# Attention masks: q minus k formed on TensorE, 1024 columns a mask instruction, middle value parts on VectorE

## The chip, the core and the metric

One core of a Trainium2 chip runs one program with five engines, each with its own in-order queue: TensorE (PE; its weight loads are shown as PEld), VectorE (DVE), ScalarE (ACT), GpSimd (POOL) and SyncE (SP), which here issues DMAs. Engines wait for each other on semaphores. The metric is the device time of one execution in microseconds (us); lower is better.

## The reference

Four blocks follow each other, each added to a residual stream after a layer norm: an attention without softmax (16 batches of 256 tokens, 16 heads of 8), a mixture of 32 experts, an RWKV block and a mixture of 8 experts. Only the first is changed. Cut to what matters:

```python
q_proj, k_proj = proj(q), proj(k)          # gelu(x @ W1 + b1) @ W2 + b2: one number a token and head
std = sqrt(0.5 * (var_q + var_k) + eps)    # over the tokens of a batch
q_proj, k_proj = (q_proj - mean_q) / std, (k_proj - mean_k) / std
Z = concatenate([k_proj, q_proj]); idx = argsort(Z)
vc = v - mean(v)                           # v centred over the tokens
# prefix sums in sorted order, read at the query positions:
context = q * sum(vc[k <= q]) - sum((vc * z)[k <= q])
norm = 2 * (q * count(k <= q) - sum(z[k <= q])) - (q * T - sum(z))
context = 2 * context / max(norm, 1e-4)
```

So each query needs sums of 18 columns a head (8 values, a 1, 8 values times k, k) over the keys that are not above it. The kernel makes a 0/1 mask of keys by queries for each head and multiplies it with these columns on TensorE. The columns go in as three bf16 parts (high, middle, third), so that their sum has float32 accuracy.

## The kernel before

`build` runs `attention0`, `routed` (32 experts), `rwkv` and `routed` (8 experts), each as blocks of five hand-written engine programs with a barrier between blocks. `attention0` has two blocks.

The first block: VectorE takes row statistics of x and writes normed rows to `h_tok` (`normed`, L498), a half (16 tiles of 128x128) at a time; TensorE turns them, makes q and k, turns those to feature-major; then a loop over 8 groups of 512 tokens (`step`, L411 to L433) multiplies by Wv, W1 and W2. The product with W2 lands on 64 partitions of one PSUM tile for q (`down["q"]`) and of another for k, and VectorE adds b2 to each and takes statistics (L559 to L567). v is centred by VectorE (L549) and turned back by TensorE. In this block GpSimd fills four small tiles (L373 to L377), and ScalarE fills `pick` and 64 rows of `q_parts` (L439 to L444). SyncE loads weights, then clears the sorted-row buffers of later blocks.

The second block begins with a preparation: VectorE turns the statistics into 1/std, then a loop over 16 batches writes `qn` and `kn` (L631, L633), TensorE turns them (L829), ScalarE copies `q_parts`, a rounded `hi_r` and the token-major `q_tok`, `k_tok` (L708 to L713), and GpSimd writes the rest of q (L762). After that TensorE sums k (L834).

Then comes the main loop, one pass a batch, software-pipelined by one batch. For four heads at a time (a quad) TensorE spreads q over all 128 partitions: four matmuls with `pick` as weights (L850) fill a 128x1024 PSUM tile. Quads 0 and 1 become masks on VectorE, one compare of 128x1024 for each half of the keys (L651). Quads 2 and 3 become masks on ScalarE, a Sign of 128x256 for each head and half of the keys (L735), with values -1, 0, 1; for these heads the columns are weighted by a half (`head_weight`, `part_weight`) and TensorE adds a matmul by ones (L867). 64 matmuls of 128x54 (L876) multiply masks and value parts, VectorE sums the three parts (L662), GpSimd forms numerators (L797, L799), and VectorE divides and takes statistics (`results`, L672 to L683). Beside that GpSimd makes the next batch's columns and their remainders (L776 to L789), and ScalarE writes the high and the middle bf16 part (L742, L749). All this stands in register loops of two batches. The order in each queue is as written in `step` and the loops: for VectorE masks of quad 0, sums of the batch before, masks of quad 1, results of the batch before; GpSimd's numerators stand just ahead of them in time.

## Time and profile before

| | us |
|---|---|
| three runs | 1201.04, 1202.76, 1203.92 (median 1202.76) |
| span of the profiled execution, first to last instruction | 1200.0 |
| first block of the attention, to the start of the group loop | 60.4 |
| group loop | 44.5 |
| second block, preparation | 26.1 |
| second block, main loop and its end | 171.5 |
| everything after the attention | 897.6 |

A span leaves out what lies before the first and after the last instruction; the profile gives no time of its own for that execution beside the span, so the median of the runs stands 2.76 us above the span. In the rows below times are us from the start of the span, unless ns is named. A row of the timeline has start, duration, engine, line, operation, output and inputs, count, and in brackets the idle time before it with what ended it. Several instructions in a row are merged (x4), and their duration runs from the start of the first to the end of the last.

### The profile page before, as it was taken

How to read it: one execution, taken by the hardware profiler on the slowest of the kernel's cores; microseconds unless marked ns; L12 is line 12 of the kernel's file. 1: busy time of each engine (PE TensorE's matmuls, PEld its weight loads, DVE VectorE, ACT ScalarE, POOL GpSimd, SP SyncE). 2: the span in 40 equal slices, each digit the busy share in tenths (PEclk: the TensorE clock that was granted, in tenths of full speed). 3: DMA queues.
4: the chain of work that ended last, by engine and by line, in shares of the span. 5: the costliest groups of instructions: out<-in, count | busy, mean ns of one | idle time of the engine just before them, and what ended most of it. 6: DMA issues, size and time to landing. Idle time of an engine off the chain costs nothing. (4 is left out here: it accounts for less than half of the span.)

```text
span 1200.0 us, 20045 instructions
## 1 busy us (share of the span) xinstructions
PE 872.6 (73%) x5732; PEld 699.2 (58%) x5732; DVE 765.0 (64%) x2389; ACT 658.5 (55%) x1352; POOL 513.8 (43%) x634
## 2 busy tenths in 40 slices
PE   3796567675238999986995366777668989999910
PEld 2633455554227889975993133444457979999900
DVE  5479688887775457212676799998868641115636
ACT  4355777776635225653664676776775645555500
POOL 0002555555226666667774773000005663035155
PEclk9998777777557999997997688798867999999965
DMA  7960000000601126645763110000031133223132
GB/s 210 289 181 0 1 0 0 0 0 1 249 17 41 47 65 193 194 139 161 197 166 95 49 49 18 1 0 1 1 142 46 43 113 91 65 82 89 40 97 61
DMA packets 133845, 97.01 MB, mean 81 GB/s; under 512 B 11649, under 2 KB 125697, under 8 KB 132737
## 3 DMA queue, kind: packets, MB, share of 16 engines
q1 hardware_dynamic: 121472, 70.79, 19.7%
q0 software_dynamic: 12288, 25.19, 7.2%
q8 instruction: 42, 0.69, 0.2%
q14 instruction: 43, 0.34, 0.1%
HBM read 45.61 MB, written 50.33 MB: 80 GB/s over the span
## 5 line engine op out<-in xcount | busy, mean ns | idle before, releaser
L1122 POOL DMA_INDIRECT e_xs<-h_tok,rows_of x128 | 128.4, 1003 | 104.1 <-DVEq L1615 35.4
L735 ACT ACTIVATE mask<-ps_q,k_neg 128x256 bf16<-128x256 f32 x256 | 100.7, 488 | 34.8 <-PE ps_q L850 34.8
L1135 POOL DMA_INDIRECT e_got<-e_ys,e_rows_of x64 | 66.2, 1035 | 115.6 <-DMA e_ys<-e_y_rows 87.5
L850 PE MATMUL ps_q<-q_parts,pick 128*128 (+1 forms) x256 | 59.2, 367 | 50.0 <-DVE mask L651 41.6
L1778 DVE TENSOR_TENSOR e_hidden<-e_ps_gu,e_hidden 128x512 f32<-128x512 f32 x48 | 33.2, 691 | 96.8 <-ACT e_hidden L1461 96.6
L1271 PE MATMUL e_ps_gu<-e_w_all,e_x_turned 128*128 x384 | 92.0, 383 | 0.1
L1466 ACT ACTIVATE e_hidden<-e_ps_up 128x512 f32<-128x512 f32 x80 | 47.8, 597 | 73.4 <-PE e_ps_up L1309 73.2
L1122 POOL DMA_INDIRECT e_xs<-h_tok,e_rows_of x64 | 66.3, 1035 | 49.7 <-DVEq L1615 19.8
L1326 PE MATMUL e_ps_y<-e_w_all,e_h_turned 128*128 x640 | 84.2, 275 | 0.0
L2283 POOL DMA_INDIRECT c_got<-e_ys,rows_of x64 | 69.8, 1090 | 30.3 <-issue 19.2
L651 DVE TENSOR_TENSOR mask<-ps_q,k_tok 128x1024 bf16<-128x1024 f32 x64 | 75.1, 1214 | 9.2 <-PE ps_q L850 7.2
L850 PEld LDWEIGHTS ps_q<-q_parts,pick 128*128 128x128 f32 x256 | 45.0, 245 | 57.2 <-issue 40.0
L1326 PEld LDWEIGHTS e_ps_y<-e_w_all,e_h_turned 128*128 128x128 f32 x640 | 77.6, 192 | 0.0
L1271 PEld LDWEIGHTS e_ps_gu<-e_w_all,e_x_turned 128*128 128x128 f32 x384 | 70.0, 192 | 8.4 <-issue 0.7
L1135 POOL DMA_INDIRECT e_got<-e_ys,rows_of x64 | 65.1, 1017 | 21.3 <-issue 17.4
L1098 POOL MEMSET e_ones_bf<- 128x128 bf16 x2 | 0.4, 204 | 156.8 <-POOLq L1904 154.5
L1461 ACT ACTIVATE e_hidden<-e_ps_gu 128x512 f32<-128x512 f32 x48 | 28.7, 598 | 55.5 <-PE e_ps_gu L1271 55.5
L2322 PE MATMUL c_ps_f<-c_f_mix_k,c_ffn_Wk 128*128 128x512 f32 x64 | 44.4, 832 | 16.7 <-DVE c_f_mix_k L1959 15.3
L2295 PE MATMUL c_ps_t<-ident,y_tok 128*128 128x128 f32 x64 | 13.1, 339 | 57.0 <-ACT y_tok L2216 29.4
L1793 DVE COPY e_y_rows<-e_ps_y 128x512 f32<-128x512 f32 x20 | 13.8, 691 | 62.4 <-PE e_ps_y L1326 62.4
L1290 PE MATMUL e_ps_ring<-e_w_all,e_h_turned 128*128 x384 | 50.8, 276 | 0.0
L662 DVE TENSOR_REDUCE sums<-ps_o 128x144 f32<-128x432 f32 x64 | 34.4, 599 | 23.0 <-PE ps_o L876 23.0
(410 smaller groups left out, 2597.4 us busy)
## 6 DMA issues: line engine op xcount, KB each, us to landing
e_x_rows<-e_xs SPq DMA_DIRECT2D x68, 256.0 KB, 2.9
e_ys<-e_y_rows SPq DMA_DIRECT2D x68, 256.0 KB, 2.4
e_xs<-zeros SPq DMA_DIRECT2D x2, 6144.0 KB, 34.2
e_w_all<-in_w SPq DMA_DIRECT2D x4, 1536.0 KB, 13.0
e_xs<-zeros SPq DMA_DIRECT2D x2, 2560.0 KB, 27.5
e_w_all<-in_w SPq DMA_DIRECT2D x4, 1024.0 KB, 11.0
x_tok<-in_x SPq DMA_DIRECT2D x4, 512.0 KB, 6.0
e_xs<-h_tok,rows_of POOLq DMA_INDIRECT x128, 2.3
```

The source lines that it names most:

```text
L651: last = nc.vector.tensor_tensor(mask[parity][quad][j][:, :].rearrange("p (h t) -> p h t", t=T), psq[0][:, :].rearrange("p (h t) -> p h t" ...
L662: last = nc.vector.tensor_reduce(sums[:, o:o + HALF * VC].rearrange("p (h r) -> p h r", r=VC), pso[u * 2 + half][:, 0:HALF * HV].rearrange ...
L735: last = nc.scalar.activation(mask[u][QS // 2 + j][keys][:, h * T:(h + 1) * T], psq[1][:, h * T:(h + 1) * T], ACT.Sign, bias=k_neg[u][:, k ...
L850: last = nc.tensor.matmul(psq[0 if on_dve else 1][:, h * T:(h + 1) * T], pick[:, (quad * HQ + h) * P:(quad * HQ + h + 1) * P], q_parts[:, ...
L1122: nc.gpsimd.indirect_dma_start(out=xs[part], out_offset=bass.IndirectOffsetOnAxis(ap=rows_of[:, t * K + k:t * K + k + 1], axis=0), in_=til ...
L1135: nc.gpsimd.indirect_dma_start(out=got[t % GB][:, k * P:(k + 1) * P], out_offset=None, in_=ys[part], in_offset=bass.IndirectOffsetOnAxis(a ...
L1271: last = nc.tensor.matmul(ps_gu[n % 2][:, t * 2 * P:(t + 1) * 2 * P], x_turned[n % 2][:, t * P:(t + 1) * P], at(w_all, col, 2 * P), start= ...
L1290: last = nc.tensor.matmul(bank_y(n)[:, o], h_turned[n % TB][:, o], at(w_all, col + 2 * P, P), start=True, stop=True)
L1326: last = nc.tensor.matmul(bank_y(q)[:, t * P:(t + 1) * P], h_turned[n % TB][:, i * P:(i + 1) * P], at(w_all, col + (CH1 + i) * P, P), star ...
L1466: nc.scalar.activation(hidden[n % HB][:, :], ps_up[n % 2][:, :], ACT.Silu).then_inc(t_hidden, 1)
L2283: nc.gpsimd.indirect_dma_start(out=got[t % GB][:, k * P:(k + 1) * P], out_offset=None, in_=env["ys0"], in_offset=bass.IndirectOffsetOnAxis ...
L2322: last = nc.tensor.matmul(ps_f[j % 2][:, :], mats["ffn_Wk"][:, i * P:(i + 1) * P], f_mix["k"][:, :], start=True, stop=True)
```

## The change

q and k are kept in one tile: W2's products go to partitions 0 to 63 (q) and 64 to 127 (k) of one PSUM tile, and are added to b2, measured and normed together. Both variances are added by one small matmul with the constant `both`. In chunks of two batches ScalarE writes a rounded copy `hi_r` (zero or negated, by row), GpSimd adds it to the value (`parts`), SyncE stores the 128x512 tile to a DRAM tensor and loads 16 pieces of it back into `q_wide` and `k_wide`. In these, each strip of 32 partitions has four rows in use: two for the parts of k (with -1 opposite) and two for the parts of q (with 1 opposite), so that a matmul over 32 rows gives q minus k for 128 keys and 256 queries. GpSimd fills the constants of these tiles in the first block. A ScalarE mask is one Sigmoid of 128x1024 with a scale of 2 to the 60. Quads 1 to 3 go to ScalarE (six such units a batch), quad 0 to VectorE, which compares q with k as before. VectorE, no longer ScalarE, copies the middle value parts; VectorE's results come two batches late instead of one. The weights of a half, the matmuls by ones, `pick` and `q_parts` are gone. Sums are taken in two halves of eight heads, with one PSUM bank for each half of the queries. The loops are written out for all 16 batches instead of register loops. PSUM: two tiles of 128x1024 for ScalarE (`psa`), one for VectorE (`psd`), two banks for the products.

Cut to what is spoken of below:

```diff
-        q_parts = sb("q_parts", N, F32R)
-        pick = sb("pick", HEADS * P, F32R)
...
+        q_wide, k_wide = ([sb(f"{n}_wide{i}", SLOTS * 2 * CW, F32R) for i in range(2)] for n in "qk")
...
                 @block.gpsimd
...
+                    def constant(ins):
+                        ins.then_inc(consts_made, 1)
+                        pool.wait_ge(consts_made, next(made))
...
+                    for x in (*q_wide, *k_wide, q_only):
+                        constant(nc.gpsimd.memset(x[:, :].bitcast(F32), 0.0))
+                    for r in range(RG):
+                        rows = slice(r * HR, r * HR + 4)
+                        for i in range(2):
+                            constant(nc.gpsimd.memset(q_wide[i][rows, :].bitcast(F32), -1.0))
+                            constant(nc.gpsimd.memset(k_wide[i][rows, :].bitcast(F32), 1.0))
+                        constant(nc.gpsimd.memset(q_only[rows, :].bitcast(F32), 1.0))
+                        constant(nc.gpsimd.memset(q_only[r * HR:r * HR + 2, :].bitcast(F32), 0.0))
...
-                                nc.tensor.matmul(down[x][0:PR, :], w2[:, :], gelu[x][:, :],
+                                nc.tensor.matmul(down[ROWS_OF[x], :], w2[:, :], gelu[x][:, :],
...
+                        nc.vector.tensor_scalar(at(proj, g * GW, GW), down[:, :], b2[:, :], None,
+                                                ALU.add).then_inc(pr_sb, 1)
...
+                @block.sync
+                def _(sp):
+                    def store(c):
+                        sp.wait_ge(parts_made, FROM + c + 1)
+                        sp.dma_start(parts_of[:, c * CW:(c + 1) * CW], parts[c % 2][:, :].bitcast(F32)).then_inc(
+                            parts_stored[c % 2], 16)
...
+                    def load(c):
+                        sp.wait_ge(parts_stored[c % 2], FROM + 16 * (c // 2 + 1))
...
+                        for g in range(RG):
+                            for x, dst, row in ((0, q_wide, 2), (1, k_wide, 0)):
...
+                                for slot in range(SLOTS):
+                                    sp.dma_start(to[:, slot], src[x][:, g, slot]).then_inc(wide_in[c % 2], 16)
...
+                    store(0)
+                    load(0)
+                    store(1)
+                    load(1)
+                    for c in range(2, CHUNKS):
+                        store(c)
+                    for c in range(2, CHUNKS):
+                        load(c)
...
                 @block.vector
...
+                    for b_ in range(NB):
+                        nc.vector.tensor_scalar(at(proj, b_ * T, T), at(proj, b_ * T, T), at(pmeans, b_, 1), at(rs, b_, 1),
+                                                ALU.subtract, ALU.mult).then_inc(normed, 1)
...
+                    def middle_part(tile):
+                        dve.wait_ge(rest_ready, FROM + tile + 1)
+                        nc.vector.tensor_copy(part(tile)[:, :, 1, :], by_head(rest, tile)).then_inc(mid_ready, 1)
...
+                    for n in range(NB + 2):
+                        if n < NB:
+                            mask_of(n, 0)
+                        if 0 <= n - 1 < NB:
+                            sums_in(n - 1, 0)
+                        if n < NB:
+                            mask_of(n, 1)
+                            middle_part(n * TPB)
...
+                        if 0 <= n - 1 < NB:
+                            sums_in(n - 1, 1)
+                        if n < NB:
+                            middle_part(n * TPB + 1)
+                        if n >= 2:
+                            results(n - 2)
...
                 @block.scalar
...
+                    for c in range(CHUNKS):
+                        act.wait_ge(normed, FROM + BPC * (c + 1))
...
+                        act.wait_ge(parts_made, FROM + max(c - 1, 0))
+                        nc.scalar.activation(hi_r[c % 2][:, :], at(proj, c * CW, CW), ACT.Copy,
+                                             scale=low_rows[:, :]).then_inc(hi_made, 1)
+                        act.wait_ge(qk_ps, FROM + c + 1)
...
+                    def steep(b_, i):
+                        act.wait_ge(q_ps_act, FROM + UNITS * b_ + i + 1)
+                        nc.scalar.activation(mask[b_ % 2][1 + i // TPB][i % TPB][:, :], psa[i % 2][:, :], ACT.Sigmoid,
+                                             scale=SHARP).then_inc(masks_act, 1)
...
+                    for b_ in range(NB):
+                        steep(b_, 0)
+                        high_part(b_ * TPB)
+                        steep(b_, 1)
+                        high_part(b_ * TPB + 1)
+                        steep(b_, 2)
...
                 @block.gpsimd
...
+                    for c in range(CHUNKS):
+                        pool.wait_ge(hi_made, FROM + c + 1)
+                        if c >= 2:
+                            pool.wait_ge(parts_stored[c % 2], FROM + 16 * (c // 2))
+                        nc.gpsimd.tensor_tensor(parts[c % 2][:, :], at(proj, c * CW, CW), hi_r[c % 2][:, :].bitcast(F32),
+                                                ALU.add).then_inc(parts_made, 1)
...
+                    for n in range(NB + 1):
+                        if n < NB:
+                            columns(n * TPB)
+                            columns(n * TPB + 1)
+                            remainder(n * TPB)
+                            remainder(n * TPB + 1)
+                            third_part(n * TPB)
+                        if n >= 1:
+                            numerators(n - 1)
+                        if n < NB:
+                            third_part(n * TPB + 1).then_inc(vals_ready, 1)
...
                 @block.tensor
...
+                    def spread(dst, b_, quad, keys):
+
+                        c, o = b_ // BPC % 2, b_ % BPC * T
+                        for i in range(2):
+                            for pair in (2 * quad, 2 * quad + 1):
+                                rows = slice(pair % RG * HR, (pair % RG + 1) * HR)
+                                first = (pair // RG * 2 + i) * CW + o
+                                weights = q_only[rows, :] if keys is None else \
+                                    k_wide[c][rows, first + keys * P:first + (keys + 1) * P]
+                                at_ = (pair % 2 * 2 + i) * T
+                                last = nc.tensor.matmul(dst[:, at_:at_ + T], weights, q_wide[c][rows, first:first + T],
+                                                        start=True, stop=True)
...
+                    def for_act(b_, i):
+                        pe.wait_ge(masks_act, FROM + max(UNITS * b_ + i - 1, 0))
+                        spread(psa[i % 2], b_, 1 + i // TPB, i % TPB).then_inc(q_ps_act, 1)
...
                             pe.wait_ge(vals_ready, FROM + b_ + 1)
...
                         if now:
-                            spread_q(b_, 0)
+                            for_act(n, 0)
                         if before:
-                            mask_values(b_ - 1, 1 - parity, 0)
-                            mask_values(b_ - 1, 1 - parity, 1)
+                            mask_values(n - 1, 0)
                         if now:
-                            spread_q(b_, 2)
+                            for_act(n, 1)
+                            for_act(n, 2)
                         if before:
-                            mask_values(b_ - 1, 1 - parity, 2)
-                            mask_values(b_ - 1, 1 - parity, 3)
+                            mask_values(n - 1, 1)
                         if now:
-                            spread_q(b_, 1)
-                            spread_q(b_, 3)
-                    pipelined(pe, NB, step)
+                            for_act(n, 3)
+                            for_act(n, 4)
+                            if n + 1 < NB:
+                                for_dve(n + 1)
+                            for_act(n, 5)
```

## Rows read from the trace of the kernel before

**Rows 1.** Stages by the windows view: stretch, length, busy time by engine, clock.

```profile
0.00:60.39 60.39, 34.55 (x160) 27.59 (x160) 31.11 (x118) 23.66 (x29) 1.06 (x10) 1.00 0.87 250
60.39:104.88 44.49, 40.53 (x112) 15.34 (x112) 36.55 (x97) 21.66 (x33) 0.05 (x1) 1.00 0.40 119
104.88:130.93 26.05, 12.62 (x69) 9.00 (x69) 20.31 (x51) 18.29 (x66) 15.15 (x30) 0.87 0.00 0
130.93:302.38 171.45, 112.47 (x1344) 89.77 (x1344) 135.60 (x227) 123.56 (x336) 93.18 (x191) 0.73 0.00 0
```

**Rows 2.** Timeline, first block: norming of the first half, next work after it.

```profile
15.74 4.20 DVE L498 TENSOR_SCALAR h_tok<-x_tok,mean,rstd 128x128 f32<-128x128 f32 x16
25.38 0.69 DVE L507 TENSOR_TENSOR qk_tok<-ps,b_qk 128x512 f32<-128x512 f32 x1 [3.89 <-PE ps L393]
```

**Rows 3.** Timeline, two places: GpSimd and VectorE instructions that meet.

```profile
303.29 0.50 POOL L1103 MEMSET e_flow<- 128x480 f32 x1
303.48 0.34 DVE L169 TENSOR_SCALAR mean<-mean 128x32 f32<-128x32 f32 x1
...
116.28 0.82 POOL L762 TENSOR_TENSOR q_parts<-qn,hi_r 32x256 f32 x1 [0.56 <-ACT hi_r L710]
116.44 0.81 DVE L633 TENSOR_SCALAR kn<-proj_k,pmeans,pvars 64x256 f32 x1
```

**Rows 4.** Groups by line and form, GpSimd: count, busy us, mean ns, idle.

```profile
L1103 POOL MEMSET e_flow<- 128x480 f32 x1 | 0.5, 497 | 0.0
L276 POOL MEMSET ident<- 128x128 f32 x1 | 0.2, 204 | 4.2 <-POOLq L118 4.2
```

**Rows 5.** Timeline, main loop, GpSimd: numerators, the second waiting for the first.

```profile
239.47 0.70 POOL L797 TENSOR_TENSOR num<-sums,q_tok 128x288 f32<-128x288 f32 x1 [0.18 <-DVE sums L662]
240.25 0.78 POOL L799 TENSOR_TENSOR num<-num,sums 128x288 f32<-128x288 f32 x1
```

**Rows 6.** Timeline, group loop, TensorE: a product with W1, then W2.

```profile
66.59 1.02 PE L419 MATMUL ps<-y_tok,w_W 128*128 x2
67.54 1.07 PE L425 MATMUL ps<-gelu_q,w 128*64 128x512 f32 x2
```

**Rows 7.** Timeline, preparation: the first norming instruction of the second block.

```profile
109.28 0.40 DVE L631 TENSOR_SCALAR qn<-proj_q,pmeans,pvars 64x256 f32 x1 [0.47 <-DVE pvars L206]
```

**Rows 8.** SyncE's DMA issues in the timeline; a store's size and landing time.

```profile
10.96 0.42 SPq L356 DMA_DIRECT2D b_bv<-in_bv  x1
11.43 0.43 SPq L356 DMA_DIRECT2D b_b<-in_b  x1
...
e_ys<-e_y_rows SPq DMA_DIRECT2D x68, 256.0 KB, 2.4
```

**Rows 9.** Groups by line and form, main loop, VectorE.

```profile
L651 DVE TENSOR_TENSOR mask<-ps_q,k_tok 128x1024 bf16<-128x1024 f32 x64 | 75.1, 1214 | 9.2 <-PE ps_q L850 7.2 <-issue 2.0
L662 DVE TENSOR_REDUCE sums<-ps_o 128x144 f32<-128x432 f32 x64 | 34.4, 599 | 23.0 <-PE ps_o L876 23.0
```

**Rows 10.** Timeline, end of the main loop, VectorE: results of the last batch.

```profile
300.59 0.21 DVE L672 TENSOR_TENSOR n<-num,half_counts 128x32 f32<-128x32 f32 x1 [1.66 <-POOL num L799]
...
301.89 0.49 DVE L683 BATCH_NORM_STATS2 stats<-y_tok 128x6 f32<-128x128 f32 x2
```

**Rows 11.** Groups by line and form, ScalarE, two sizes without a bias tile.

```profile
L2211 ACT ACTIVATE c_ex<-c_ex 128x2048 f32<-128x2048 f32 x8 | 15.3, 1910 | 0.3
...
L2185 ACT ACTIVATE c_r<-c_ps_kvr 128x512 f32<-128x512 f32 x8 | 4.8, 597 | 9.0 <-PE c_ps_kvr L2305 9.0
```

**Rows 12.** Timeline, main loop, TensorE: spreads of q and products of masks.

```profile
130.93 2.07 PE L850 MATMUL ps_q<-q_parts,pick 128*128 128x256 f32 x8 [0.47 <-ACT k_sum L719]
...
146.65 0.74 PE L850 MATMUL ps_q<-q_parts,pick 128*128 x4 [0.68 <-ACT mask L735]
...
160.87 1.66 PE L876 MATMUL ps_o<-vals,mask 128*128 128x54 bf16 x32
...
262.16 1.22 PE L850 MATMUL ps_q<-q_parts,pick 128*128 x4 [3.00 <-DVE mask L651]
```

## What the change should do to the time

> **What bounds the kernel now.** I read the cores first (one core), then busy time by stage [rows 1], then the timeline of each stage that the change touches. Only the attention changes: 302.4 us, four stages with four limits. In the first block no engine is busy for more than about half of the 60.4 us: TensorE and VectorE wait for each other in turn, and what ends last there is VectorE's norming and TensorE's turns, one after the other. In the group loop TensorE is busy for 40.5 of 44.5 us, at a granted clock of 1.00: TensorE is the bound, and VectorE's 36.6 lie beside it. The preparation is a chain of small steps over the batches. The main loop takes 171.45 us, nearly 10.2 for each of the first 15 periods if about 9 us are given to either end. VectorE is busy for 135.6 of it, 8.5 a batch; its rest is waiting for q in PSUM and for products [rows 9]. TensorE's clock is 0.73 in the mean: after a wait of 3.00 us for a mask four spread matmuls take 1.22, after one of 0.68 they take 0.74 [rows 12], so the engine runs at the lower level (1.2 GHz) after long waits. GpSimd's 93.2 are 5.8 a batch.
>
> **First block: +21.5 us (0 to +23).** What is new here is GpSimd's work: twenty memsets of 2048 columns and about a dozen small ones. From 204 ns for 128 columns and 497 for 480 [rows 4] a column is 0.83 ns, so one of 2048 takes 0.204 + 1.6 = 1.8; with 0.08 between two that wait for each other [rows 5], 1.88. Four of 128 rows come first, then four times four of four rows, with small ones between; the cost goes by columns. GpSimd would start at about 10.6, when SyncE too begins with this block [rows 8], and be busy to about 51.
>
> It has nothing else to do, but VectorE is held up. Where a tensor_scalar of VectorE met a GpSimd instruction, it did not end before it: a compute on 32 columns, begun 0.19 after a memset, ended at 303.82, the memset at 303.79; a norming of 256 columns that takes 0.40 undisturbed [rows 7] took 0.81 and ended 0.15 after GpSimd's [rows 3]. VectorE's `normed` on `h_tok` is sixteen of these in 4.20 [rows 2], and the root ahead of it has four. If each waits for the memset that runs, one gets through a gap. The four cost some 4.6 in all, so norming starts at 20.35 instead of 15.74; sixteen more against eleven large memsets and five small ones (11 × 1.88 + 5 × 0.3 = 22.2) end at 42.5, where now they end at 19.94. That is +22.6, and one microsecond comes back, because the turns of the earlier groups, now partly waiting, are done by then. The 3.89 of idle time before the next VectorE work [rows 2] doesn't absorb it: it is a wait for TensorE, which starts from the last normed tiles. Later norming has slack. If two instructions pass in each gap it is +14; if none waits, 0. I take +21.5, by the two meetings.
>
> **Group loop: −1.9 us (−4.3 to 0).** One bias add instead of two and fewer statistics save VectorE 1.3 us a group, which TensorE hides; it shows after the last matmul only, −0.9. q's and k's products with W2 go to different columns of the array now; a pair takes 1.07 [rows 6], and if the two overlapped this would give 0.43 a group, 3.4 in all. I take −1.0, since nothing here shows two such matmuls beside each other.
>
> **Preparation: +8.9 us (+4 to +14).** SyncE now stands in the chain. Norming starts at 4.4 after the block's start [rows 1, 7]; two batches, ScalarE's rounding (0.6 for 512 columns, [rows 11]) and GpSimd's sum (1.5, from 0.82 for 256 columns, [rows 3]) make the first `parts` ready at about +7.5. The store of a 256 KB tile lands after 2.4; an issue takes 0.42 and comes 0.47 after the one before [rows 8], so the sixteen of `load(0)` take 7.5. Behind them on SyncE's queue stand `store(1)`, another 2.5, and `load(1)`, another 7.5: `store(2)` is issued at about +28. For that GpSimd's fifth `parts` waits, whose buffer it frees, then `store(3)` and the sixth, and ScalarE's roundings behind those, and so the last `q_tok` and `k_tok`, for which TensorE waits before it sums k. That makes about +34, and +35 for the first spread, now +26.05 [rows 1]. The lower bound stands for stores that land sooner and shorter issues, the upper one for pieces that land late. From the third chunk on a load (7.5 and 2.5) has two batches of time, about 17, to hide in.
>
> **Main loop: −25.9 us.** Work a batch on each engine:
> VectorE: two masks of 1.214 and sums of 4 × 0.599 minus a little for fewer, larger pieces [rows 9], 2.34 + 2.15; two middle copies, 0.6 together; results 1.79 [rows 10]: 6.9.
> ScalarE: six masks. 512 columns take 597 ns, 2048 take 1910 [rows 11], so a column takes 0.855 ns, 1024 take 1.03 and the 288 of a high part 0.4: 6.2 and 0.8 are 7.0.
> GpSimd: numerators 0.70 + 0.78 [rows 5] and columns, remainders and third parts as now: 5.8 to 6.2.
> TensorE: 28 spread matmuls, 0.11 to 0.21 each by the forms of 256 columns, and 64 products at 0.85 (estimate at the upper clock, half of the lower) or 1.66 for 32 [rows 12]: 4.8 at the upper level, up to 9.2 at the lower.
> None of these is 8.5, but two things add to them. First, VectorE's middle copy and its results come now when GpSimd forms numerators and the third part, and those of VectorE's instructions that behave as in [rows 3] wait for 0.70 or 0.78 at a time: +0.9 to 1.8. Second, a ring runs through four engines: products of one half, spreads between, products of the other half, the last sums (1.1), numerators (1.5), the third part (0.7), then the next products: 6.0 at the upper clock, 8.0 at the lower. TensorE waits in each period, and so I expect it at the lower level much of the time. I take 8.5 a period (7.2, ScalarE and its waits alone, to 9.5, TensorE at the lower level): 9 for the start, 15 × 8.5, 9 for the end are 145.5, against 171.45.
>
> A rule of the Trainium skill speaks against the change. A switch from 128x128 to 128x64 matmuls shows 0.09 between the last of the one and the first of the other [rows 6], nothing that the sum has to hold. The Trainium skill, "TensorEngine Tiling (Array Packing)", Key Properties, says that a change of tiling mode drains TensorE; by it, six changes a batch at 0.09 would be 9 us of TensorE's time in all, an estimate, which lies beside other work unless TensorE is the bound. The Trainium skill, "TensorE: Matmul & The Clock Gate", Part 3, says for the other side that matmuls of 32 rows in different row groups run beside each other; no row here shows such matmuls. By it the lower-level case would have a period of 8.2 to 8.5, not 9.5.
>
> **The sum.** 21.5 − 1.9 + 8.9 − 25.9 = +2.6 on the span of 1200.0, and 2.8 for what lies around it (the median of the runs against the span): 1205.4.
>
> **The rivals.**
> The memsets hold VectorE up little or not at all, because the meetings in [rows 3] were chance or because a gap lets all through: the first block stays as it is, and the rest gives 1200 − 1.9 + 8.9 − 25.9 + 2.8 = 1184, faster. For it: only two meetings carry the term, both of other shapes. Against it: both agree to within 0.15.
> The loop is bound by TensorE at the lower clock: the 32-row spreads cost as much as those of 128 rows, the period is 9.5, and with the first block held up the time is 1205.4 + 15 = 1220. For it: the clock of 0.73 and the 3 us waits [rows 1, 12]. Against it: fewer waits for VectorE's masks, of which two are left of four.
> The loop is bound by ScalarE alone, and nothing collides in it: 7.2 a period, 1205.4 − 19.5 = 1186, faster. For it: six masks are the longest single sum. Against it: the ring is longer at the lower clock.
> Break-even is a period of 8.3 with the first block held up, and 9.7 without.
>
> **How the numbers follow.** Forecast 0.45, memsets harmless 0.22, TensorE's bound 0.18, ScalarE's bound 0.10, anything else (a preparation far longer, or all gains at once) 0.05. A measurement can tell about 0.2% from no change, 2.4 us. The forecast's own range is 1196 to 1215: of its 0.45, 0.27 is slower, 0.08 the same, 0.10 faster. With the harmless memsets (0.21 faster, 0.01 the same), TensorE's bound (0.18 slower), ScalarE's (0.10 faster) and the rest (0.04 faster, 0.01 the same) that is faster 0.45, the same 0.10, slower 0.45. Range: 1179 to 1221; it leaves out the lower edge of the harmless case, the upper edge of TensorE's bound and most of the rest, about 0.16.
>
> **What would show it.** First block: MEMSETs of 1.8 us on GpSimd from 10.6 to 51 and the sixteen `h_tok` instructions stretched from 4 to some 22 us, each ending with a memset; if they still take 4.20, the first term falls. Preparation: SyncE's issues 0.47 apart, VectorE's or ScalarE's first mask at about +36 of the block. Loop: a period of 8 to 9; GpSimd's numerators ending where VectorE's middle copy or results end; a clock under 0.8 if the ring is slow. The prediction is wrong if memsets of four rows cost less than those of 128 rows, if the loads of the pieces land many microseconds late, or if the ring isn't what a period waits for.

## The result, and the profile after

The changed kernel takes 1190.97 us (median of four runs, 1189.72 to 1192.21) against 1202.37 for the kernel before: a ratio of 0.9905, 95% interval 0.9891 to 0.9919. It is faster by 11.4 us, where 2.6 us slower was forecast. The span of the profiled execution is 1187.6 us. Its stages, by the windows view (start and end of the stretch; its length; busy time and count of TensorE, its weight loads, VectorE, ScalarE, GpSimd; granted clock, share of the DMA engines, GB/s), in the order of [rows 1]:

```profile
0.00:79.31 79.31, 35.93 (x160) 27.84 (x160) 49.30 (x118) 18.29 (x28) 39.90 (x43) 0.96 0.88 254
79.31:118.40 39.09, 35.18 (x112) 13.45 (x112) 25.61 (x72) 20.46 (x33) 0.00 (x0) 1.00 0.02 7
118.40:147.35 28.95, 10.70 (x40) 7.83 (x40) 11.14 (x34) 7.71 (x24) 9.88 (x8) 0.50 0.18 64
147.35:290.83 143.48, 108.02 (x1473) 86.91 (x1472) 114.83 (x227) 104.87 (x130) 97.48 (x195) 0.50 0.04 11
290.83:1187.60 896.77, 673.71 (x4046) 558.41 (x4048) 539.72 (x1897) 470.85 (x889) 406.31 (x404) 0.85 0.28 85
```

Read the lengths against [rows 1]: the first block is 18.9 us longer, the group loop 5.4 shorter, the preparation 2.9 longer, the main loop 28.0 shorter, the rest 0.85 shorter. That is -12.4 on the span.

**First block.** VectorE in the timeline (start, duration, engine, line, operation, output and inputs, count), then GpSimd's fills of 128 rows and of four, where [rows 2] stood before:

```profile
14.92 1.78 DVE L187 TENSOR_SCALAR spread<-spread 128x16 f32<-128x16 f32 x1
20.74 13.75 DVE L513 TENSOR_SCALAR h_tok<-x_tok,mean,rstd 128x128 f32<-128x128 f32 x16
...
44.97 1.61 DVE L506 TENSOR_SCALAR spread<-rstd 128x16 f32<-128x16 f32 x1
46.62 1.82 DVE L196 TENSOR_SCALAR rstd<-spread 128x16 int32<-128x16 int32 x1
50.83 1.11 DVE L513 TENSOR_SCALAR h_tok<-x_tok,mean,rstd 128x128 f32<-128x128 f32 x4
...
65.68 0.69 DVE L522 TENSOR_TENSOR qk_tok<-ps,b_qk 128x512 f32<-128x512 f32 x1 [8.88 <-PE ps L415]
```

```profile
11.13 3.67 POOL L391 MEMSET q_wide<- 128x2048 f32 x2
...
28.72 1.83 POOL L396 MEMSET k_wide<- 4x2048 f32 x1
30.61 1.83 POOL L395 MEMSET q_wide<- 4x2048 f32 x1
```

Sixteen norming instructions take 13.75 us instead of 4.20, about two to a fill of 1.83. A fill of four rows costs as much as one of 128: two of those take 3.67. In the root (VectorE's way to 1/std, ahead of the norming), tensor_scalars of 16 columns that take 0.17 us without a fill last 1.6 to 1.8, in the second half of the tiles as in the first. Not every VectorE instruction is held: the root's last nine, from 18.86 to 20.70, none of them a tensor_scalar, take 0.17 to 0.18 each, as they do without a fill, beside one that runs from 18.85 to 20.64. In the kernel before, a tensor_scalar of the root, the second half's norming and the use of its first product stood here:

```profile
13.03 0.17 DVE L187 TENSOR_SCALAR spread<-spread 128x16 f32<-128x16 f32 x1
...
33.62 1.11 DVE L498 TENSOR_SCALAR h_tok<-x_tok,mean,rstd 128x128 f32<-128x128 f32 x4
...
46.78 0.69 DVE L507 TENSOR_TENSOR qk_tok<-ps,b_qk 128x512 f32<-128x512 f32 x1 [7.19 <-PE ps L393]
```

**Group loop.** TensorE, the products with W2, where [rows 6] stood before:

```profile
86.34 0.65 PE L447 MATMUL ps<-gelu_q,w 128*64 128x512 f32 x1
86.35 0.64 PE L447 MATMUL ps<-gelu_k,w 128*64 128x512 f32 x1
...
86.83 0.59 PE L447 MATMUL ps<-gelu_k,w 128*64 128x512 f32 x1
```

q's and k's product start 0.01 us apart and run beside each other; the last of the four matmuls ends at 87.42.

**Preparation.** SyncE's issues (pairs are merged):

```profile
125.47 0.36 SPq L643 DMA_DIRECT2D qk_parts<-parts  x1
127.51 0.59 SPq L660 DMA_DIRECT2D q_wide<-qk_parts  x2
128.15 0.55 SPq L660 DMA_DIRECT2D k_wide<-qk_parts  x2
...
134.37 0.53 SPq L660 DMA_DIRECT2D q_wide<-qk_parts  x2
...
139.58 8.44 SPq L643 DMA_DIRECT2D qk_parts<-parts  x6
```

The pieces are issued 0.30 us apart, not 0.47 as in [rows 8], and the first store is known to have landed 2.0 after its issue, when the first piece is issued. The last line is the chain's turning point: the third store, and five more, stand behind 32 pieces.

**Main loop.** One period (8.37 us, from one start of the first half's products to the next), put together from the timelines of TensorE, VectorE and GpSimd:

```profile
205.72 1.60 PE L914 MATMUL ps_o<-vals,mask 128*128 128x54 bf16 x32 [0.37 <-ACT mask L783]
207.25 0.81 PE L882 MATMUL ps_a<-q_wide,k_wide 32*128 32x256 f32 x8
207.35 1.12 DVE L713 TENSOR_REDUCE sums<-ps_o 128x144 f32<-128x432 f32 x2 [0.80 <-PE ps_o L914]
208.53 1.62 PE L914 MATMUL ps_o<-vals,mask 128*128 128x54 bf16 x32 [0.48 <-DVE sums L713]
210.19 1.12 DVE L713 TENSOR_REDUCE sums<-ps_o 128x144 f32<-128x432 f32 x2 [0.37 <-PE ps_o L914]
211.39 0.70 POOL L837 TENSOR_TENSOR num<-sums,q_tok 128x288 f32<-128x288 f32 x1 [0.31 <-DVE sums L713]
212.17 0.82 POOL L839 TENSOR_TENSOR num<-num,sums 128x288 f32<-128x288 f32 x1
212.95 0.88 POOL L826 TENSOR_TENSOR vals<-rest,vals 128x288 bf16<-128x288 f32 x1
214.09 1.60 PE L914 MATMUL ps_o<-vals,mask 128*128 128x54 bf16 x32 [0.38 <-ACT mask L783]
```

Each of these starts where another ends, across three engines: products, sums, products, sums, numerators, third part, next products. The last line names ScalarE's mask as what ended its wait: the six masks and the third part are done within 0.1 us of each other. The 32 products take 1.60 us, 1.66 in [rows 12]; the clock is 0.50, the lower level, in the preparation and the whole loop.

### The profile page after: what moved, and what is told of

Read it like the earlier page. It is cut to its first block and busy times, and to the rows that moved or that the text cites. A ratio compares the mean times of both kernels' runs of the same rounds, so it can differ in the third digit from the quotient of the medians.

```text
span 1187.6 us, 19422 instructions
## 1 busy us (share of the span) xinstructions
PE 863.5 (73%) x5828; PEld 694.4 (58%) x5830; DVE 740.6 (62%) x2348; ACT 622.2 (52%) x1104; POOL 553.6 (47%) x649
## 5 line engine op out<-in xcount | busy, mean ns | idle before, releaser
L1160 POOL DMA_INDIRECT e_xs<-h_tok,rows_of x128 | 129.1, 1009 | 103.1 <-DVEq L1653 35.4
L783 ACT ACTIVATE mask<-ps_a 128x1024 bf16<-128x1024 f32 x96 | 94.3, 1020 | 28.5 <-PE ps_a L882 28.5
L882 PE MATMUL ps_a<-q_wide,k_wide 32*128 32x256 f32 x384 | 57.0, 494 | 15.0 <-ACT mask L783 13.2
L914 PE MATMUL ps_o<-vals,mask 128*128 128x54 bf16 x1024 | 51.5, 225 | 15.1 <-DVE sums L713 8.5
L914 PEld LDWEIGHTS ps_o<-vals,mask 128*128 128x128 bf16 x1024 | 47.4, 122 | 23.9 <-DVE sums L713 12.2
L882 PEld LDWEIGHTS ps_a<-q_wide,k_wide 32*128 32x128 f32 x384 | 37.9, 307 | 27.3 <-ACT mask L783 25.1
```

Source lines behind the costliest of these rows:

```text
L783: nc.scalar.activation(mask[b_ % 2][1 + i // TPB][i % TPB][:, :], psa[i % 2][:, :], ACT.Sigmoid, scale=SHARP).then_inc(masks_act, 1)
L882: last = nc.tensor.matmul(dst[:, at_:at_ + T], weights, q_wide[c][rows, first:first + T], start=True, stop=True)
L914: last = nc.tensor.matmul(pso[ic][:, h * HV:(h + 1) * HV], mask[b_ % 2][head // HQ][j][:, o:o + P], vals[b_ % 2][:, vo:vo + HV], start=(j ...
L1160: nc.gpsimd.indirect_dma_start(out=xs[part], out_offset=bass.IndirectOffsetOnAxis(ap=rows_of[:, t * K + k:t * K + k + 1], axis=0), in_=til ...
```

## The experiments

All times below are medians of four or more runs; ratios are against the kernel before on the chip of that run, where it took 1202.04 to 1205.04. The stages by the windows view, in us:

| kernel | first block | group loop | preparation | main loop | time | ratio |
|---|---|---|---|---|---|---|
| before | 60.39 | 44.49 | 26.05 | 171.45 | 1202.37 | |
| after | 79.31 | 39.09 | 28.95 | 143.48 | 1190.97 | 0.9905 |
| e1 | 60.02 | 39.08 | 28.85 | 143.44 | 1169.61 | 0.9723 (0.9707 to 0.9739) |
| e2 | 80.13 | 39.09 | 18.88 | 144.70 | 1181.24 | 0.9829 (0.9812 to 0.9845) |
| e3 | 60.00 | 44.39 | | | 1202.33 | 0.9998 (0.9985 to 1.0011) |
| e4 | 77.93 | 39.04 | 28.96 | 141.71 | 1186.30 | 0.9879 (0.9860 to 0.9898) |
| e5 | 62.71 | 60.12 | 28.83 | 143.46 | 1193.94 | 0.9907 (0.9877 to 0.9937) |
| e6 | 81.19 | 39.05 | 29.06 | 140.74 | 1189.09 | 0.9866 (0.9841 to 0.9891) |
| e7 | 60.51 | 39.04 | 19.01 | 142.22 | 1164.10 | 0.9661 (0.9634 to 0.9687) |
| e9 | 77.95 | 46.95 | 28.95 | 143.28 | 1197.52 | 0.9934 (0.9910 to 0.9957) |
| e10 | 60.41 | 39.03 | 18.81 | 143.43 | 1161.02 | 0.9671 (0.9651 to 0.9691) |
| e11 | 60.48 | 39.05 | 18.84 | 144.74 | 1166.32 | 0.9710 (0.9694 to 0.9726) |
| e12 | 60.70 | 39.10 | 22.20 | 140.52 | 1162.14 | 0.9669 (0.9653 to 0.9685) |
| e13 | 60.01 | 39.04 | 18.72 | 125.90 | 1143.91 | 0.9509 (0.9494 to 0.9525) |

Where fills and norming meet, the first block varies by itself, 77.9 to 81.2 us in five profiles of the same code; small differences are read from the stage, not from the total.

**e1: constants by ScalarE.**

```diff
-                    for x in (*q_wide, *k_wide, q_only):
+                    for x in (*sign_rows.values(), q_only):
                         constant(nc.gpsimd.memset(x[:, :].bitcast(F32), 0.0))
...
-                            constant(nc.gpsimd.memset(q_wide[i][rows, :].bitcast(F32), -1.0))
...
+                        constant(nc.gpsimd.memset(sign_rows["q"][rows, :], -1.0))
...
+                        if g == GPH - 1:
+                            for x, tiles in (("q", q_wide), ("k", k_wide)):
+                                for t in tiles:
+                                    nc.scalar.activation(
+                                        t[:, :].rearrange("p (r c) -> p r c", c=P),
+                                        ones[:, :].unsqueeze(1).broadcast_to([P, SLOTS * 2 * CW // P, P]), ACT.Copy,
+                                        scale=sign_rows[x][:, :]).then_inc(consts_made, 1)
```

> The changed kernel with its twenty constant fills of 2048 columns taken off GpSimd: ScalarE writes the four tiles whole, one copy of a tile of ones with a scale by row each (four of some 1.9 us), between its fourth and its fifth copy of h, where it is idle for 18 us. Theory (VectorE's norming waits for whatever fill GpSimd has running): the first block goes from 79.3 back to about 60.4 us, the sixteen norming instructions from 13.75 to about 4.2, the time from 1191 to about 1172. Rival (the first block is longer for another reason: two more weight loads, the fills' writes as such, the lower clock): it stays near 79 and the time within 3 us of 1191.

Measured: 1169.61 us; the first block is 60.02. Timeline of e1, VectorE's norming and ScalarE's first two constants (the other two take 3.88 as well):

```profile
16.11 4.19 DVE L520 TENSOR_SCALAR h_tok<-x_tok,mean,rstd 128x128 f32<-128x128 f32 x16
...
22.99 3.88 ACT L468 ACTIVATE q_wide<-ones,sign_q 128x2048 fp32r<-128x2048 f32 x2
```

The norming takes 4.19 again and all 19.3 us of the stage come back. The fills, and nothing else that the change adds to the block, had made it longer. Four instructions do on ScalarE what twenty did on GpSimd, since the rows' signs are in the scale.

**e5: the same fills beside the group loop.**

```diff
+                    pool.wait_ge(v_ps, FROM + 1)
                     for x in (*q_wide, *k_wide, q_only):
```

> The changed kernel with one wait more on GpSimd: the 29 fills of constants begin when TensorE has made the first product of the group loop, so the same 40 us of fills lie beside the group loop (39.1 us in the changed kernel), in which GpSimd is otherwise idle, and not beside the norming. Theory (the fills hold up VectorE's instructions wherever they meet, and in the group loop VectorE is near the bound): the first block is back at about 60.4 us (-18.9) and the group loop gets 8 to 15 us longer, since its tensor_scalars (6 a group, some 4.4 us a group) wait: time 1180 to 1187. Rival (only norming is held up, or the group loop has cover): the group loop stays under 42 us, time 1172 to 1175.

Measured: 1193.94 us. The first block is back but for some 2 us (62.71), and the group loop takes 60.12, 21.0 more; 8 to 15 were expected. Windows view of e5, then a pair of VectorE's centrings of v, 0.61 in the changed kernel:

```profile
62.71:122.83 60.12, 41.57 (x112) 15.88 (x112) 43.26 (x72) 21.16 (x33) 38.12 (x29) 0.89 0.28 83
```

```profile
65.85 3.83 DVE L565 TENSOR_SCALAR v_cent<-v_fm,vmean 128x256 f32<-128x256 f32 x2
```

In the changed kernel VectorE is busy for only 25.6 of 39.1 us there, and yet 38 us of GpSimd's work cost 21.0, a little more than beside the norming. The held instruction is the one that TensorE waits for: six waits in e5's group loop come to 16.0 us, where the changed kernel has one of 1.0. The rest is TensorE itself, busy for 41.6 us instead of 35.2 at a granted clock of 0.89 instead of 1.00; the matmuls behind the waits are the longer ones. What GpSimd's idle time is worth depended here on which of VectorE's instructions ran in it; VectorE's busy share alone didn't tell it.

**e2: the stores first.**

```diff
-                    store(0)
-                    load(0)
-                    store(1)
-                    load(1)
-                    for c in range(2, CHUNKS):
+                    for c in range(4):
                         store(c)
-                    for c in range(2, CHUNKS):
+                    load(0)
+                    for c in range(4, CHUNKS):
+                        store(c)
+                    for c in range(1, CHUNKS):
                         load(c)
```

> The changed kernel with SyncE's queue in another order: stores 0 to 3 of the parts, then the first load, then stores 4 to 7, then the other loads. Theory (the chain of the preparation runs through SyncE's queue, where stores 2 and 3 stand behind 32 issues of loads): the first spread of the main loop comes 8 to 9 us earlier, at about 20 us after the block's start instead of 28.95, and the time goes from 1191 to about 1182. Rival (the stores' landing and GpSimd's sums pace the preparation): 26 us or more after the block's start, time 1188 or more.

Measured: 1181.24 us; the preparation falls from 28.95 to 18.88. SyncE's issues in e2 and TensorE's first spread:

```profile
126.29 5.24 SPq L643 DMA_DIRECT2D qk_parts<-parts  x4
...
136.48 5.02 SPq L643 DMA_DIRECT2D qk_parts<-parts  x4
...
138.10 0.58 PE L881 MATMUL ps_d<-q_wide,q_only 32*128 32x256 f32 x2 [0.23 <-DMA k_wide<-qk_parts]
```

The queue's order was the price: with it mended the preparation is 7.2 us shorter than in the kernel before, although it moves more. Now the load ends last, 0.23 us behind TensorE's sum of k. 1.2 us of the 10.1 return in the main loop, because GpSimd still makes the last two `parts` (2.48 us from 138.67) when the loop wants its columns.

**e3 and e9: what shortened the group loop.** In e3 the kernel before gets the other 64 columns for k, and nothing else:

```diff
-            down = {"q": ps[5], "k": ps[6]}
+            down = {"q": ps[5][0:PR, :], "k": ps[6][PR:P, :]}
```

> The kernel before with one part of the change alone: k's product with W2 goes to PSUM partitions 64 to 127 (the other 64 columns of the array) and VectorE adds b2 from there; the number of VectorE instructions stays as before. Theory (q's and k's products overlap on different column halves): the two start within 0.1 us of each other, the group loop goes from 44.5 to about 40.5 us, time from 1202.4 to about 1198.4. Rival (the 5.4 us that the group loop gained come from VectorE's fewer instructions): the group loop stays at 44 to 44.5, time 1202.

Measured: 1202.33 us; the group loop is 44.39. Timeline of e3, TensorE and VectorE:

```profile
67.15 0.64 PE L425 MATMUL ps<-gelu_q,w 128*64 128x512 f32 x1
67.15 0.64 PE L425 MATMUL ps<-gelu_k,w 128*64 128x512 f32 x1
...
73.31 0.66 PE L431 MATMUL ps<-ident,v_cent 128*128 128x128 f32 x4 [0.68 <-DVEq L554]
```

```profile
69.98 0.74 DVE L566 BATCH_NORM_STATS2 pstats<-proj_q  x2
70.64 0.73 DVE L566 BATCH_NORM_STATS2 pstats<-proj_k  x2
```

The overlap is there, TensorE's busy time falls from 40.5 to 35.4, and not one microsecond is gained: TensorE now waits for VectorE, 0.68 here and 5.2 us in eight waits, while VectorE's instructions follow each other almost without a gap. The theory (-4) falls; the rival's number came out, but the overlap isn't idle in the changed kernel, as the rival had it. Before the change two chains of nearly the same length, 5.03 us a group on TensorE and as much on VectorE, lay beside each other; the overlap alone shortens one. The changed kernel shortens both and gains 5.4. SyncE's transfers are no rival: they lie under the group loop of the kernel before (DMA share 0.40) and hardly under that of the changed kernel (0.02), but in e1 they lie there again, and the loop is as short. Windows view of e1:

```profile
60.02:99.10 39.08, 35.19 (x112) 13.47 (x112) 25.61 (x72) 20.46 (x33) 0.00 (x0) 1.00 0.51 151
```

e9 was to show the other half, VectorE's saving without the overlap: k's product stands behind the turns of v.

> The changed kernel with k's product with W2 moved behind the turns of v, so that it no longer stands beside q's on TensorE; VectorE's work as in the changed kernel. Theory (TensorE and VectorE each allow some 4.9 to 5.0 us a group before the change, so that the overlap alone, or VectorE's saving alone, gives next to nothing, and both together 0.6 a group): the group loop goes from 39.1 back to 43 to 44.5 us, time 1195 to 1196. Rival (VectorE's fewer instructions give the most): the group loop stays at 39 to 41, time 1191 to 1193.

Measured: 1197.52 us, group loop 46.95, longer than before the change. The products take 1.07 each again, but VectorE's add now waits 2.00 us in each group for k's product behind the turns. The edit put a wait of its own into the chain, so e9 shows that the overlap matters in the changed kernel (+7.9 without it) and not how much VectorE's saving alone would give.

**e4: the third part first.** GpSimd's order changes so, and VectorE's and ScalarE's middle and high parts move ahead with it:

```diff
                             third_part(n * TPB)
+                            third_part(n * TPB + 1).then_inc(vals_ready, 1)
                         if n >= 1:
                             numerators(n - 1)
-                        if n < NB:
-                            third_part(n * TPB + 1).then_inc(vals_ready, 1)
```

> The changed kernel with the third value part taken off the ring: GpSimd makes both third parts ahead of the numerators of the batch before, VectorE copies both middle parts ahead of its second sums, ScalarE makes both high parts ahead of its second mask. Theory (the period of 8.37 is a ring: products 1.6, sums 1.1, products 1.6, sums 1.1, numerators 1.6, third part 0.9, and the next products): numerators and third part leave the ring, the period falls to 7.2 to 7.5, where ScalarE's six masks and TensorE's products in turn hold it; the time goes from 1191 to 1174 to 1178. Rival (the period is VectorE's work and its waits for GpSimd): the period stays at 8.1 to 8.4, time 1187 to 1191.

Measured: 1186.30 us; main loop 141.71, period 8.24. Only 0.13 a period is gained. Timeline of e4, a period from TensorE and ScalarE:

```profile
206.58 1.62 PE L912 MATMUL ps_o<-vals,mask 128*128 128x54 bf16 x32 [0.48 <-DVE sums L713]
208.13 0.81 PE L880 MATMUL ps_a<-q_wide,k_wide 32*128 32x256 f32 x8
208.97 3.85 ACT L782 ACTIVATE mask<-ps_a 128x1024 bf16<-128x1024 f32 x4 [0.90 <-PE ps_a L880]
212.00 1.60 PE L912 MATMUL ps_o<-vals,mask 128*128 128x54 bf16 x32 [0.25 <-issue]
```

Numerators and third part are off the chain, and a second ring of nearly the same length takes over: second-half products, a spread, three of ScalarE's masks, first-half products, first sums.

**e6: products split.** e4, with the first half waiting for the two masks of ScalarE that it reads:

```diff
                             for_act(n, 0)
-                        if before:
-                            mask_values(n - 1, 0)
-                        if now:
                             for_act(n, 1)
-                            for_act(n, 2)
                         if before:
                             mask_values(n - 1, 1)
                         if now:
+                            for_act(n, 2)
                             for_act(n, 3)
...
                             for_act(n, 5)
+                            mask_values(n, 0)
...
-                            pe.wait_ge(masks_act, FROM + UNITS * (b_ + 1))
+                            pe.wait_ge(masks_act, FROM + UNITS * b_ + TPB)
                             pe.wait_ge(vals_ready, FROM + b_ + 1)
+                        else:
+                            pe.wait_ge(masks_act, FROM + UNITS * (b_ + 1))
```

> e4 with TensorE's order changed too: the first half's products wait only for the masks they read (two of ScalarE's six) and stand behind the sixth spread of their own batch; the second half's products stand behind the second spread of the next batch. Theory (with the third part off the ring the period of 8.24 is held by a second ring, second-half products 1.6, spread, ScalarE's masks 3, 4 and 5 at 0.95 each, first-half products 1.6, sums 1.1): no engine waits for all six masks any more, ScalarE's masks run on end, and the period falls to 7.2 to 7.6, where VectorE's own 7.2 us of work are next; time 1171 to 1177. Rival (TensorE at the lower clock is the bound, with 4.8 to 6.5 us of work a period and its switches): the period stays above 8.0, time 1183 or more.

Measured: 1189.09 us; main loop 140.74, periods of 8.0 and 8.5 in turn. The theory's 7.2 to 7.6 did not come, and what holds this order's period was not shown. From 180 to 260 us TensorE is busy for 69.8 of 80 us and VectorE for 74.5:

```profile
180.00:260.00 80.00, 69.80 (x908) 57.59 (x904) 74.47 (x135) 62.64 (x79) 56.70 (x117) 0.50 0.04 10
```

**e11: middle parts back on ScalarE.** e7 (e1, e2 and e6 together, below), with `middle_part` moved to ScalarE:

```diff
                         steep(b_, 1)
+                        middle_part(b_ * TPB)
+                        middle_part(b_ * TPB + 1)
                         steep(b_, 2)
```

> e7 with the middle value parts copied by ScalarE again, between its second and third mask; VectorE copies none. Theory (in e7's order the period of 8.0 is VectorE's: 7.4 of 8.0 us busy, of which the two middle copies are 1.05 since they wait for GpSimd): the period falls by 0.5 to 0.9, the time from 1164 to 1151 to 1157. Rival (TensorE at the lower clock is the bound; it is busy for 7.0 of 8.0): the period stays at 7.9 to 8.2, time 1161 to 1166.

Measured: 1166.32 us; main loop 144.74, period 8.34. VectorE is busy 14.5 us less in the loop (110.80 against 125.26 in e7) and nothing is gained; TensorE and ScalarE now wait for each other in turn (1.25 and 0.86 in a period). VectorE alone was not the bound in e7's order either, and VectorE's copying of the middle parts is worth no more than 2.5 us of the loop there (142.22 with it, 144.74 without).

**e12: TensorE busy ahead of the loop.** e10 with thirteen products that nobody reads in the preparation (one of the three places where they stand):

```diff
+                        nc.tensor.matmul(psa[0][:, 0:GW], ones[:, :], v_tok[:, 0:GW], start=True, stop=True)
```

> e10 with thirteen products of ones that nothing reads, on TensorE in the preparation, so that it is busy ahead of the main loop. Nothing of the result is left out. Theory (the lower clock, 0.50 in the preparation and the whole main loop, is what makes the products 1.6 instead of 0.85 and so the ring 8.2 long): where the clock is at the upper level the 32 products take 0.8 to 0.9 and a period 6.8 to 7.4; if it holds through the loop, 12 us or more less than e10, if it falls again in the first periods, within 3 us of e10. Rival (the period is not TensorE's): periods at the upper clock are as long as at the lower.

Measured: 1162.14 us, 1.1 from e10. Windows view of e12, preparation, first four microseconds of the loop, next eight, and TensorE at the change:

```profile
99.80:122.00 22.20, 17.79 (x66) 10.16 (x66) 12.10 (x34) 9.37 (x26) 10.20 (x8) 0.85 0.21 82
122.00:126.00 4.00, 1.99 (x21) 1.33 (x20) 3.46 (x5) 3.40 (x5) 3.39 (x12) 0.89 0.33 121
126.00:134.00 8.00, 6.74 (x98) 5.43 (x98) 6.17 (x10) 6.54 (x9) 5.23 (x12) 0.50 0.04 11
```

```profile
123.67 0.50 PE L891 MATMUL ps_a<-q_wide,k_wide 32*128 32x256 f32 x4 [0.93 <-ACT mask L788]
125.25 1.49 PE L891 MATMUL ps_a<-q_wide,k_wide 32*128 32x256 f32 x6 [1.07 <-ACT mask L788]
```

At the upper level (2.4 GHz) four spreads take 0.50, not 0.80. The clock falls after two waits of about 1 us for ScalarE's masks, before the first products of values, and stays at 0.50. Being busy before the loop doesn't hold the clock in it; the preparation is 3.4 us longer, the loop 2.9 shorter. No products of masks and values at the upper level were seen in it.

**e13: half of the products left out.** So their price was changed in another way:

```diff
-                                for j in range(TPB):
+                                for j in range(1):
```

> e10 with half of the products of masks and value parts left out: only the first 128 keys of each batch are multiplied, 16 products a half and not 32, so the attention's sums lack the other keys. At the lower clock 16 products take 0.8 us, about what 32 would take at the upper one. Theory (e4's and e10's period of 8.24 is a ring through TensorE at the lower clock: both halves' products 1.6 each, spread, three of ScalarE's masks): the period falls by 0.8 to 1.2, to 7.0 to 7.4, where VectorE's 7.2 us of work are next; time 1143 to 1149. Rival (ScalarE's and VectorE's own chains hold the period): it stays above 7.9, time 1156 or more.

Measured: 1143.91 us; main loop 125.90, period 7.23. Windows view of e13:

```profile
180.00:230.00 50.00, 37.12 (x420) 28.07 (x420) 49.04 (x97) 45.09 (x57) 40.66 (x84) 0.50 0.03 8
```

With products of 0.88 to 0.90 instead of 1.60 the period falls by 1.0, as the theory has it, and VectorE is next, busy for 49.0 of 50 us. So the period of 8.24 runs through TensorE's products, and VectorE's 7.2 lie right behind. What the clock has to do with their 1.60 is seen in the kernel before, whose main loop runs at both levels. Windows view of it, two stretches that each hold one set of 32 products from its first start to its last end (and two matmuls more that reach into it):

```profile
144.40:145.41 1.01, 1.01 (x34) 1.01 (x33) 0.00 (x0) 1.01 (x5) 0.19 (x1) 0.96 0.00 0
160.87:162.53 1.66, 1.66 (x34) 1.66 (x34) 1.16 (x4) 0.24 (x1) 0.74 (x1) 0.50 0.00 0
```

Such a set takes 1.66 at the lower level and 1.01 near the upper one, more than the 0.8 to 0.9 that was taken for it in the prediction and before e12 and e13. A loop of the changed kernel at the upper level was not run.

**e7 and e10: the causes together.** e7 is e1, e2 and e6; e10 is e1, e2 and e4.

> The constants by ScalarE (e1), the stores first (e2) and the products split (e6) together in the changed kernel. If the three causes are separate stages, the gains add: -21.4, -9.7 and what e6 shows, some -14 to -19: 1141 to 1147 if e6 goes as its theory says, 1152 to 1156 if it stays at e4's time.

> The changed kernel with the constants by ScalarE (e1), the stores first (e2) and the third part first (e4). The three act in three stages, so the gains add: -21.4 - 9.7 from 1191 are 1160, and e4's main loop was 1.8 us shorter than the changed kernel's (141.7 against 143.5): 1156 to 1160. If e7's order of products is the better one it stays behind 1164.

Measured: 1164.10 and 1161.02 us, ratios of 0.9661 and 0.9671, which can't be told apart. The gains of e1 and e2 add nearly in full, since they lie in different stages (0.9723 and 0.9829 against 0.9905 make 0.9648). The loop's new orders, worth 1.8 us in e4 and 2.7 in e6, give most of that back: the main loop is 143.43 in e10 and 142.22 in e7, where it starts, as in e2, while GpSimd still makes the last two `parts`. By this e10 misses its expected 1156 to 1160; e7 misses both its ranges, 1141 to 1147 and 1152 to 1156. Both beat the kernel before by more than 3%, some 41 us, three times and more what the change itself gives.

Which part of the change makes the main loop 28.0 us shorter than in the kernel before is not shown: no run has the kernel before with one of these parts. The runs show what the new period consists of.

## Why the prediction was wrong

The mechanisms were those of the trace, nearly all of them; four sizes were off, all of them to the same side. By the prediction's own terms:

| term | predicted | measured |
|---|---|---|
| first block | +21.5 (0 to +23) | +18.9 |
| group loop | -1.9 (-4.3 to 0) | -5.4 |
| preparation | +8.9 (+4 to +14) | +2.9 |
| main loop | -25.9 | -28.0 |
| after the attention | 0 | -0.85 |
| outside the span | 2.8 | 3.4 |

Together they are 14.4 us less than 1205.4. The time lies inside the range (1179 to 1221), outside the forecast's own range of 1196 to 1215, and on the other side of no change.

**Preparation, 6.0 of the 14.4.** The chain was right: the third store behind 32 issues of loads, GpSimd's fifth `parts` and ScalarE's roundings behind it, the first spread last; e2 shows it by taking it away. The step that failed is "an issue takes 0.42 and comes 0.47 after the one before": the rows were loads of biases, [rows 8], and a piece of two rows is issued 0.30 after the one before. Sixteen take 4.8 and 5.2 us and not 7.5, which is 5.0 of the 6.0; the stores, known to have landed after 2.0 instead of 2.4, give most of the rest. Another kind of transfer was taken as if it were the same; the lower bound (+4) didn't reach down to the measured +2.9 either.

**Group loop, 3.5.** The step that failed is "VectorE 1.3 us a group, which TensorE hides" together with a discount on the overlap to 1.0 of 3.4. The overlap came in full (q's and k's products together from 86.34 to 87.42, 1.08, where [rows 6] has 1.07 for one of them). Even in full it gives nothing alone (e3); with VectorE's saving beside it, 5.4 come. So that saving was not hidden by TensorE, as the prediction had it, but let the overlap count; what it gives alone is not shown, since e9 put a new wait into the chain. The windows gave a hint: VectorE was busy for 36.6 and TensorE for 40.5 of 44.5 [rows 1]; with 5 us off TensorE, VectorE is the longer one once its waits are counted. Two edits that shorten two near-equal chains have to be priced as one.

**First block, 2.6, and right partly by accident.** The mechanism stands on e1 and e5: VectorE's tensor_scalars wait for the fill that runs, four rows cost as much as 128, norming starts 5.0 late (4.6 predicted; 0.4 of the 5.0 are statistics that start later). Two steps failed against each other. "If each waits for the memset that runs, one gets through a gap" put the norming's end 22.6 late; two go through a gap, 16 in 13.75, and it is 14.6 late, which the text had as its other value, "If two instructions pass in each gap it is +14". "Later norming has slack" is wrong: the three held instructions in the second root delay the second half's norming from 13 us late to 17 (50.83 against 33.62), and its first product is used 18.9 late. The rival "memsets harmless" fell. The Trainium skill, "SBUF — State Buffer", section Who interferes with whom, says that a VectorE instruction in a two-port mode and a GpSimd instruction exclude each other for the whole of an instruction; the trace agrees, up to 1.8 us at a time, in e5 too.

**Main loop, 2.1.** A period of 8.5 was predicted and 8.37 measured, and the predicted ring stands in the rows of the period; e4 shows a second ring of nearly the same length beside it, and e13 that the period runs through TensorE's products. The rival "TensorE's bound" with 9.5 fell, since the 32-row spreads are cheap: eight, on four strips of rows, take 0.81, and four on two take 0.80. The Trainium skill, "TensorE: Matmul & The Clock Gate", Part 3, was right that they run beside each other. The Trainium skill, "TensorEngine Tiling (Array Packing)", Key Properties, spoke of a drain at a change of mode; the spreads at 207.25 begin before the products' modelled end at 207.32, so no price of it shows here. "ScalarE's bound" with 7.2 fell too. Inside the ring a step was wrong: between the two halves' products stand not the spreads but the first sums (1.1), because both halves use the same banks. VectorE's collisions with GpSimd are there (0.69 for 0.21 at `results`), but off the ring, so by these rows they cost nothing in the changed kernel; in e13, where VectorE is busy for 49.0 of 50 us, they would count. The 0.85 for 32 products at the upper level was half of the lower-level row; the kernel before shows 1.01. The changed loop did not run at that level.

**The chances.** The forecast sat 2.6 above no change because four terms were each taken dearer than they proved. The chance of 0.45 for faster and the wide range came from the doubts about the first block and the period, and those terms were the good ones; that the time lies inside the range is partly luck, since what had widened it did not come true.

## What to carry to other kernels

Price an issue, a fill or a copy from a row of its own shape, and where only another shape has a row, put the range around it and not on one side. Before work is given to an idle GpSimd, look at which VectorE instructions will meet it and who waits for those: the same 38 us cost 19 us beside the norming and 21 beside a loop in which VectorE had a third of its time free, and nothing when ScalarE did them in 7.8. Where two chains lie within a tenth of each other, as here, shortening one can give nothing. An order that freed one ring uncovered the next; what all rings share, here TensorE's products, is where a lower cost showed in the period (e13).

## What the runs showed of the hardware that was not expected

- GpSimd's fill of 2048 columns takes 1.81 us on 128 rows and on 4; two VectorE tensor_scalars of 128 columns go through between two fills, and the root's tensor_tensors beside a fill are held only where they stand behind a held tensor_scalar.
- Products of 64 columns on different halves of the array, started 0.01 us apart, run beside each other: q's and k's take 1.08 together, and 1.07 each where they stand apart (e9).
- TensorE went through the whole main loop of the changed kernel, and of each variant, at the lower level (0.50); where it entered the loop at the upper one (e12), it fell after waits of 0.93 and 1.07 us for masks and did not rise again. 32 products of 54 columns take 1.66 us at 0.50 and 1.01 at 0.96 (the kernel before).
